# Moving the out-attention's score matmuls by a quarter of a projection, with its copies and its diagonal moved on ScalarE and GpSimd

## The chip, the cores and the metric

The kernel runs on 1 core of one Trainium2 chip. The metric is device microseconds of one execution. Five engines work beside each other, each through its own instructions in order: TensorE (PE in the profile; its weight loads are PEld), VectorE (DVE), ScalarE (ACT), GpSimd (POOL) and SyncE (SP, which here only starts transfers). They meet at semaphores: an instruction adds to one when it is done, another engine waits until it has reached a count.

## The reference

A stack of four graph layers works on 128 graphs of 64 nodes with 512 features, in float32. Layer 1, where the change lies, is

```
Wh  = x @ W[h]                      for 4 heads, 512 -> 512 each
e   = leaky(f1[:, None] + f2[None, :]),  f1 = Wh @ a[h][:512], f2 = Wh @ a[h][512:]
h   = elu(softmax(masked e) @ Wh)   heads side by side: 2048 wide
out = the same attention once more, one head, W_out: 2048 -> 512, a_out, elu
y   = relu(out @ w1 + b1) @ w2 + b2 + out, normalised, added to x, normalised
```

The first attention is the kernel's `at` (names `ah_...` in the profile), the second, the out-attention, is `ao_` (names `ao_...`).

## The kernel before, in words

A tile is 128 rows, that is two graphs; there are T = 64 tiles, worked in 32 pairs. Layer 1 runs as a pipeline over pairs: each engine has a function `step(p)`, written for p = 0 and 1, then a loop for p = 2 to 29, then p = 30 and 31. In one step TensorE aggregates and projects pair p head by head (k = 4p + head), multiplies the heads of pair p by W_out (`out_part`), and does the out-attention of the pair before, m = p - 1 (tiles 2m and 2m + 1), as well as the head attention of the pair after (tiles 2p + 2 and 2p + 3). The order on every engine is written out by hand; nothing reorders it.

TensorE's order in a step, with the lines the profile names:

- `project(p, 0, 0)`, `project(p, 0, 1)` (L2012). A projection has two quarters in each call, s = 0 and s = 1, 12 matmuls each, and ends with `h_done`.
- `out_part(m, 3, c)` (L2026), which finishes the previous pair's sums over heads in `wop` (`wo_done`); then `at.pe_scores(2p + 3)` (L212).
- `project(p, 1, 0)`; then the wait for `ao_.diag_ready` and `ao_.pe_scores(2m)` (L101); `project(p, 1, 1)`.
- `aggregate(p, 1)` (L1992), whose second bank first waits for `ao_.summed`; `out_part(p, 0, c)`; then `banks_free(p, 1)`, a wait until VectorE has read all four parts of the aggregate (`y_lo_ready`), and the turns `at.pe_turn` (L268) and `ao_.pe_turn(2m)` (L148).
- `project(p, 2, 0)`; `ao_.pe_scores(2m + 1)` (L101); `project(p, 2, 1)`; `out_sums(2m)` (L2034); `out_part(p, 1, c)`; a wait for `att_ready` and the turns of 2m + 1 and 2p + 3; `project(p, 3, *)`; `aggregate(p + 1, 0)`; `out_part(p, 2, c)`; `out_sums(2m + 1)`; `at.pe_scores(2p + 4)` (L212).

What feeds a score of the out-attention is a chain over the other engines. ScalarE copies `wop` to `who` (`keep_wo`, L1466). VectorE makes two weighted row sums of it (`out_f`, L1743 and L1747, with `ao_f` as result and `ao_.f_ready`). GpSimd spreads one of them over a diagonal (`ao_.pool_diag`, L93, `ao_.diag_ready`). TensorE then multiplies the diagonal (L101), VectorE adds, gates and masks (`dve_before_exp`, L109 to L120), ScalarE takes the exponential.

The head attention's own sums are made in between by the others: GpSimd multiplies a row tile by one of 8 vectors (`products_of`, L1300, k = 0 to 7, "product k" below), ScalarE sums each product (`dots`, L1436). There are two buffers for products, so product k waits for dot k - 2. `at.pool_diag` (L196, L199, L203) makes the head attention's diagonal, `pool_prob` (L260 for heads, L140 for the out-attention) its probabilities. In the steps p = 30 and 31 there are no products.

VectorE's order around it: `at.dve_add(2p + 3)` (L225), `out_f(2m)`, `natural` (L1765), `h_lo(k, 1)` (L1729), `ao_.dve_before_exp(2m)`, `elu(k + 1, 0)` (L1720, L1723), `at.dve_peak`, `ao_.dve_after_exp`, `elu(k + 1, 1)`, four `y_lo` (L1712), `h_lo(k + 1, 0)`, `out_f(2m + 1)`, `at.dve_after_exp`, `h_lo(k + 1, 1)`, `elu(k + 2, 0)`, `ao_.dve_before_exp(2m + 1)`, `elu(k + 2, 1)`, `out_elu(2m)` (L1753, L1756, `att_ready`). The third `y_hi` on ScalarE (L1446) waits for the first `y_lo`.

Of the kernel before, what the change touches and what calls it, by code (L numbers as in the profile page):

```python
# [415 lines left out]
def gnn_stack_kernel(nc, x, x_turned, adj, W0T, b0, Wh, ah, Wo, ao, w1, b1, w2, b2, gamma, beta,  # L416
                     W2, a2s, a2d, W3, a3s, a3d, out):
    B, N, _ = x.shape
    T = B * N // P
# [14 lines left out]
    with ExitStack() as top:  # L434
# [14 lines left out]
        same_graph = sb("same_graph", [P, P])  # L449
# [505 lines left out]
        with ExitStack() as ctx:  # L955
# [134 lines left out]
            def pair(p):  # L1090

                return not isinstance(p, int) or 0 <= p < PAIRS
# [191 lines left out]
            def _(pool):  # L1284
# [30 lines left out]
                def step(p):  # L1315
                    m = p - 1
                    first = 2 * p + 4, p + 2, 0
                    second = 2 * p + 5, p + 2, 1
                    if pair(p + 1):
                        at.pool_diag(nc, pool, 2 * p + 3, p + 1, 1, i64)  # L1320
                    if fresh(p + 2):
                        products_of(*first, range(0, 1))
                    if pair(p - 2):
                        split_att(2 * (p - 2) + 1, 1)
                    if fresh(p + 2):
                        products_of(*first, range(1, 2))
                    if pair(p + 1):
                        at.pool_prob(nc, pool, 2 * p + 2)
                    if fresh(p + 2):
                        products_of(*first, range(2, 4))  # L1330
                    if pair(m):
                        ao_.pool_diag(nc, pool, 2 * m, i64)
                    if fresh(p + 2):
                        products_of(*first, range(4, 6))
                    if pair(m):
                        ao_.pool_prob(nc, pool, 2 * m)
                    if fresh(p + 2):
                        products_of(*first, range(6, NV))
                    if pair(p + 2):
                        at.pool_diag(nc, pool, 2 * p + 4, p + 2, 0, i64)  # L1340
                    if pair(m):
                        ao_.pool_diag(nc, pool, 2 * m + 1, i64)
                    if pair(p + 1):
                        at.pool_prob(nc, pool, 2 * p + 3)
                    if fresh(p + 2):
                        products_of(*second, range(0, 2))
                    if pair(m):
                        ao_.pool_prob(nc, pool, 2 * m + 1)
                    if fresh(p + 2):
                        products_of(*second, range(2, 5))  # L1350
                    if pair(m):
                        split_att(2 * m, 0)
                    if fresh(p + 2):
                        products_of(*second, range(5, NV))
# [71 lines left out]
            def _(act):  # L1426
# [53 lines left out]
                def step(p):  # L1480
                    m = p - 1
                    k = 4 * p
                    first = 2 * p + 4, p + 2, 0
                    second = 2 * p + 5, p + 2, 1
                    if pair(m):
                        h_hi(k - 1, 1)
                    if pair(p - 2):
                        out_exp(2 * (p - 2) + 1)
                    exp(k, 0)
                    if pair(p + 1):  # L1490
                        at.act_exp(nc, act, 2 * p + 2)
                    if fresh(p + 2):
                        dots(*first, (0,))
                    if pair(p - 2):
                        split_att(2 * (p - 2) + 1, 1, p - 1)
                    exp(k, 1)
                    h_hi(k, 0)
                    if fresh(p + 2):
                        dots(*first, (1, 2))
                    if pair(m):  # L1500
                        keep_wo(m, 0)
                    h_hi(k, 1)
                    if pair(m):
                        keep_wo(m, 1)
                    if fresh(p + 2):
                        dots(*first, (3,))
                    exp(k + 1, 0)
                    if fresh(p + 2):
                        dots(*first, (4,))
                    if pair(m):  # L1510
                        ao_.act_exp(nc, act, 2 * m)
                    exp(k + 1, 1)
                    for n in range(3):
                        y_hi(p, 1, n)
                    if pair(p + 1):
                        at.act_exp(nc, act, 2 * p + 3)
                    y_hi(p, 1, 3)
                    h_hi(k + 1, 0)
                    if fresh(p + 2):
                        dots(*first, (5, 6))  # L1520
                    h_hi(k + 1, 1)
                    if pair(p + 1):
                        at.act_turned(nc, act, 2 * p + 2, p + 1, 0, agg_done)
                    if pair(m):
                        ao_.act_turned(nc, act, 2 * m)
                    if fresh(p + 2):
                        dots(*first, (7,))
                    exp(k + 2, 0)
                    if pair(m):
                        ao_.act_exp(nc, act, 2 * m + 1)  # L1530
                    if fresh(p + 2):
                        dots(*second, (0,))
                    exp(k + 2, 1)
                    if pair(m):
                        out_exp(2 * m)
                    if fresh(p + 2):
                        dots(*second, (1,))
                    h_hi(k + 2, 0)
                    if pair(m):
                        split_att(2 * m, 0, m + 1)  # L1540
                    if fresh(p + 2):
                        dots(*second, (2, 3))
                    h_hi(k + 2, 1)
                    if pair(p + 1):
                        at.act_turned(nc, act, 2 * p + 3, p + 1, 1, agg_done)
                    if pair(m):
                        ao_.act_turned(nc, act, 2 * m + 1)
                    if fresh(p + 2):
                        dots(*second, (4,))
                    exp(k + 3, 0)  # L1550
                    if fresh(p + 2):
                        dots(*second, (5,))
                    exp(k + 3, 1)
                    if pair(p + 1):
                        for n in range(3):
                            y_hi(p + 1, 0, n)
                    if fresh(p + 2):
                        dots(*second, (6,))
                    if pair(p + 1):
                        y_hi(p + 1, 0, 3)  # L1560
                    h_hi(k + 3, 0)
                    if fresh(p + 2):
                        dots(*second, (7,))
# [415 lines left out]
            def _(pe):  # L1979
# [17 lines left out]
                def banks_free(p, q):  # L1997
                    pe.wait_ge(y_lo_ready, 4 * (2 * p + q) + 4)

                def project(p, h, half):  # L2000
                    k = 4 * p + h
                    side = h % 2
                    if half == 0:
                        pe.wait_ge(y_lo_ready, 4 * (2 * p + h // 2) + 2 + 2 * side)
                    ge(pe, hv_ready, 2 * (k - 1) + half + 1)
                    for s in range(2):
                        f = slice((2 * half + s) * P, (2 * half + s + 1) * P)
                        for c in range(KC):
                            passes = split_passes(big_hi[:, h * KC + c, f], big_lo[:, h * KC + c, f],
                                                  yT[0][:, side, c, :], yT[1][:, side, c, :])  # L2010
                            for i, (a, b) in enumerate(passes):
                                ins = nc.tensor.matmul(hp[half][:, s * 2 * P:(s + 1) * 2 * P], a, b,  # L2012
                                                       start=c == 0 and i == 0, stop=c == KC - 1 and i == 2)
                    ins.then_inc(h_done, 1)
# [23 lines left out]
                def step(p):  # L2038
# [16 lines left out]
                            out_part(m, 3, c)  # L2055
                    if pair(p + 1):
                        at.pe_scores(nc, pe, 2 * p + 3, same_graph)
                    project(p, 1, 0)
                    if pair(m):
                        pe.wait_ge(at.summed, capped(2 * p + 4, T))  # L2060
                        ao_.pe_scores(nc, pe, 2 * m, same_graph)
                    project(p, 1, 1)
                    aggregate(p, 1, scores_read)
                    for c in range(KC):
                        out_part(p, 0, c)
# [3 lines left out]
                    if pair(m):  # L2069
                        ao_.pe_turn(nc, pe, 2 * m, ident)  # L2070
                    project(p, 2, 0)
                    if pair(m):
                        pe.wait_ge(ao_.turned_ready, 2 * (2 * m + 1))
                        ao_.pe_scores(nc, pe, 2 * m + 1, same_graph)
                    project(p, 2, 1)
                    if pair(m):
                        pe.wait_ge(at.turned_ready, capped(2 * (2 * p + 3), 2 * T))
                        out_sums(2 * m, 0)
# [191 lines left out]
```

## Time and profile before

| what | value |
|---|---|
| median of 3 runs | 3117.1 us (3115.95 to 3119.1) |
| the profiled execution, its own time | 3117.14 us |
| its span, first to last instruction | 3115.4 us |
| TensorE matmul, busy | 3003.0 us, 96% |
| VectorE, busy | 2262.0 us, 73% |
| GpSimd, busy | 2070.8 us, 66% |
| ScalarE, busy | 1737.4 us, 56% |
| granted TensorE clock, mean | 0.994 |

A matmul's recorded end is modelled and overlaps the next one's start, so what a stream of them takes is read from the distances of their starts. The step of pairs is the unit here: layer 1's steps repeat with the same distances, so one step is read closely and counted.

### The profile page before, as it was taken

To read this page: it belongs to the slowest core of one execution; us is meant where nothing else is said; L and a number is where in the kernel's file an instruction comes from. 1 tells how busy PE (TensorE), PEld (TensorE's weight loads), DVE (VectorE), ACT (ScalarE), POOL (GpSimd) and SP (SyncE) were. 2 spreads that over 40 slices of the span, in tenths; PEclk is the share of its full clock that TensorE was granted. 3 is DMA by queue.
4 is the path that set the end of the run, shared out by engine and by line. 5 is a ranking of instruction groups with operands and counts; after the bars stand their busy time and mean duration, and the time that the engine had idled before them with its cause. 6 is when DMAs were issued, how large, how long until landed. Compare 5 with 4: busy or idle time off the path is not lost.

```text
span 3115.4 us, 65262 instructions
## 1 busy us (share of the span) xinstructions
PE 3003.0 (96%) x19324; PEld 2656.3 (85%) x19324; DVE 2262.0 (73%) x4877; ACT 1737.4 (56%) x4250; POOL 2070.8 (66%) x2901
## 2 busy tenths in 40 slices
PE   8999989999999999999999999999799999999997
PEld 6878879888888888888888888889688888888885
DVE  7777656767676676766767667674788888888885
ACT  3333345555555555555555555553566767676675
POOL 5666656666666666666666656641588888888885
PEclk9999999999999999999999999999999999999999
DMA  6555421111111111111111111111633332333320
GB/s 200 179 187 183 148 83 34 49 51 47 44 48 49 47 47 44 53 45 47 47 44 54 44 47 47 45 50 55 193 96 95 101 93 87 99 101 99 93 74 31
DMA packets 308643, 247.65 MB, mean 79 GB/s; under 512 B 150060, under 2 KB 215644, under 8 KB 308316
## 3 DMA queue, kind: packets, MB, share of 16 engines
q1 hardware_dynamic: 296796, 221.64, 23.9%
q10 hardware_dynamic: 9216, 16.78, 1.4%
q0 software_dynamic: 2560, 8.39, 0.8%
q8 instruction: 32, 0.52, 0.1%
q14 instruction: 39, 0.32, 0.0%
HBM read 162.83 MB, written 83.91 MB: 79 GB/s over the span
## 4 chain that ended last, share of the span: by engine, by line
PE 65%; POOL 8%; issue 7%; DMA 2%; SPq 1%; DVE 1%; ACT 1%; POOLq 0%; DVEq 0%; ACTq 0%
PE wop L2026 18%; PE hp L2012 16%; PE wop L47 9%; PE hp L2145 5%; PE hp L47 5%; POOL w_first L1300 3%; PE agg L1992 2%; PE agg_b L1992 2%; DMA att_scratch<-who 2%; PE agg_b L2034 2%; PE agg_b L2112 2%; PE agg L2112 2%; SPq L1181 1%; POOL who L1305 1%; POOL g_terms L1365 1%
## 5 line engine op out<-in xcount | busy, mean ns | idle before, releaser
L1300 POOL TENSOR_TENSOR w_first<-xd,v_row 128x512 f32<-128x512 f32 x480 | 637.8, 1344 | 88.2 <-ACT w_first L1436 88.2
L2012 PE MATMUL hp<-yT_hi,big_hi 128*128 128x256 f32 x2048 | 589.8, 288 | 0.0
L2012 PE MATMUL hp<-yT_lo,big_hi 128*128 128x256 f32 x2048 | 579.3, 283 | 0.0
L2012 PE MATMUL hp<-yT_hi,big_lo 128*128 128x256 f32 x2048 | 579.0, 283 | 0.0
L1729 DVE TENSOR_TENSOR hT_lo<-ex,hT_hi 128x512 fp32r<-128x512 f32 x256 | 269.8, 1054 | 229.8 <-ACT hT_hi L1458 229.7
L2026 PE MATMUL wop<-big_hi,hT_hi 128*128 128x512 f32 x1024 | 408.3, 399 | 0.0
L2026 PE MATMUL wop<-big_lo,hT_hi 128*128 128x512 f32 x1024 | 399.9, 391 | 0.0
L2026 PE MATMUL wop<-big_hi,hT_lo 128*128 128x512 f32 x1024 | 399.9, 391 | 0.0
L2012 PEld LDWEIGHTS hp<-yT_lo,big_hi 128*128 128x128 f32 x2048 | 392.8, 192 | 0.0
L2012 PEld LDWEIGHTS hp<-yT_hi,big_hi 128*128 128x128 f32 x2048 | 392.3, 192 | 0.2
L2012 PEld LDWEIGHTS hp<-yT_hi,big_lo 128*128 128x128 f32 x2048 | 392.2, 192 | 0.0
L1436 ACT ACTIVATE w_first<-w_first 128x512 f32<-128x512 f32 x480 | 301.7, 630 | 117.2 <-POOL w_first L1300 111.2
L1365 POOL TENSOR_TENSOR g_terms<-x,g_v_row 128x512 f32<-128x512 f32 x256 | 342.2, 1357 | 33.8 <-ACT x L1587 33.8
L1458 ACT CAST hT_hi<-ex 128x512 fp32r<-128x512 f32 x256 | 158.9, 621 | 213.7 <-PE wop L2026 213.7
L1720 DVE TENSOR_SCALAR ex<-ex 128x512 f32<-128x512 f32 x256 | 125.5, 490 | 192.8 <-ACT ex L1453 191.3
L1453 ACT ACTIVATE ex<-hp 128x512 f32<-128x512 f32 x256 | 152.2, 595 | 172.1 <-PE hp L2012 169.5
L2026 PEld LDWEIGHTS wop<-big_hi,hT_hi 128*128 128x128 f32 x1024 | 192.4, 188 | 44.2
L2026 PEld LDWEIGHTS wop<-big_hi,hT_lo 128*128 128x128 f32 x1024 | 192.2, 188 | 40.7
L47 PE MATMUL wop<-w_hi,g_agg_hi 128*128 128x512 f32 x512 | 219.4, 429 | 4.5 <-DVE g_agg_lo L1836 4.3
L2026 PEld LDWEIGHTS wop<-big_lo,hT_hi 128*128 128x128 f32 x1024 | 192.5, 188 | 36.5
L47 PE MATMUL wop<-w_lo,g_agg_hi 128*128 128x512 f32 x512 | 202.3, 395 | 0.0
L47 PE MATMUL wop<-w_hi,g_agg_lo 128*128 128x512 f32 x512 | 201.7, 394 | 0.0
(219 smaller groups left out, 7969.9 us busy)
## 6 DMA issues: line engine op xcount, KB each, us to landing
x0f<-in_x_turned SPq DMA_DIRECT2D x64, 256.0 KB, 2.7
xt<-in_x SPq DMA_DIRECT2D x64, 256.0 KB, 2.9
x_scratch<-w_first ACTq DMA_DIRECT2D x64, 256.0 KB, 2.3
xa<-x_scratch SPq DMA_DIRECT2D x64, 256.0 KB, 2.7
att_hi_scratch<-att_hi SPq DMA_DIRECT2D x64, 256.0 KB, 2.0
att_lo_scratch<-who SPq DMA_DIRECT2D x64, 256.0 KB, 2.0
att_hi<-att_hi_scratch SPq DMA_DIRECT2D x64, 256.0 KB, 3.6
att_lo<-att_lo_scratch SPq DMA_DIRECT2D x64, 256.0 KB, 4.4
```

The lines of the kernel that those rows point to most:

```text
L47: ins = nc.tensor.matmul(out, a, b, start=first and c == 0 and q == 0, stop=last and c == n - 1 and q == 2)
L1300: nc.gpsimd.tensor_tensor(terms[:, k % TR, :], xd[:], v_row[:, k, :], ALU.mult).then_inc(terms_ready, 1)
L1365: nc.gpsimd.tensor_tensor(g.terms[:, k, :], x, g.v_row[:, k, :], ALU.mult).then_inc(g.terms_ready, 1)
L1436: nc.scalar.activation(terms[:, k % TR, :], terms[:, k % TR, :], ACT.Identity, accum_out=at.f[:, j, k:k + 1]).then_inc(at.f_ready[j], 1)
L1453: nc.scalar.activation(ex[half][:], hp[half][:], ACT.Exp).then_inc(ex_ready, 1)
L1458: nc.scalar.copy(hT[0][:, 2 * half:2 * half + 2, :].rearrange("p c n -> p (c n)"), ex[half][:]).then_inc(hT_hi_ready, 1)
L1720: nc.vector.tensor_scalar(ex[half][:], ex[half][:], 1.0, -1.0, ALU.min, ALU.add).then_inc(neg_ready, 1)
L1729: nc.vector.tensor_tensor(hT[1][:, own, :].rearrange("p c n -> p (c n)"), ex[half][:], hT[0][:, own, :].bitcast(F32).rearrange("p c n -> p ...
L1992: ins = nc.tensor.matmul(by_head(banks[j][:, g, :])[:, :, c, :], xa[j][own, c * P:(c + 1) * P], at.turned[own, j, 2 * q:2 * q + 2, :], sta ...
L2012: ins = nc.tensor.matmul(hp[half][:, s * 2 * P:(s + 1) * 2 * P], a, b, start=c == 0 and i == 0, stop=c == KC - 1 and i == 2)
L2026: ins = nc.tensor.matmul(wop[j][:], a, b, start=h == 0 and c == 0 and i == 0, stop=h == HEADS - 1 and c == KC - 1 and i == 2)
L2145: ins = nc.tensor.matmul(bank[:, s * 2 * P:(s + 1) * 2 * P], x, y, start=c == 0 and q == 0, stop=c == KC - 1 and q == 2)
```

## The change

Four edits.

- TensorE: `project` takes a function that it calls between its two quarters. `ao_.pe_scores(2m)` with its waits goes from before `project(p, 1, 1)` to the middle of it, and `ao_.pe_scores(2m + 1)` from before `project(p, 2, 1)` to the middle of that.
- ScalarE: in the first half of the step dot 2 moves from ahead of `keep_wo(m, 0)` to behind `keep_wo(m, 1)`, next to dot 3.
- GpSimd: `ao_.pool_diag(2m + 1)` goes ahead of `at.pool_diag(2p + 4)`.
- Nothing is added or removed: each instruction of before is issued once per step still, no transfer moves, and the epilogue behind the last step, written out apart, is as it was.

```diff
@@ GpSimd, step
                     if fresh(p + 2):
                         products_of(*first, range(6, NV))
+                    if pair(m):
+                        ao_.pool_diag(nc, pool, 2 * m + 1, i64)
                     if pair(p + 2):
                         at.pool_diag(nc, pool, 2 * p + 4, p + 2, 0, i64)
-                    if pair(m):
-                        ao_.pool_diag(nc, pool, 2 * m + 1, i64)
@@ ScalarE, step
                     if fresh(p + 2):
-                        dots(*first, (1, 2))
+                        dots(*first, (1,))
                     if pair(m):
                         keep_wo(m, 0)
                     h_hi(k, 1)
                     if pair(m):
                         keep_wo(m, 1)
                     if fresh(p + 2):
-                        dots(*first, (3,))
+                        dots(*first, (2, 3))
@@ TensorE
-                def project(p, h, half):
+                def project(p, h, half, between=None):
...
                     for s in range(2):
+                        if s == 1 and between is not None:
+                            between()
@@ TensorE, step
+                    def scores_0():
+                        if pair(m):
+                            pe.wait_ge(at.summed, capped(2 * p + 4, T))
+                            ao_.pe_scores(nc, pe, 2 * m, same_graph)
+
+                    def scores_1():
+                        if pair(m):
+                            pe.wait_ge(ao_.turned_ready, 2 * (2 * m + 1))
+                            ao_.pe_scores(nc, pe, 2 * m + 1, same_graph)
+
                     project(p, 1, 0)
-                    if pair(m):
-                        pe.wait_ge(at.summed, capped(2 * p + 4, T))
-                        ao_.pe_scores(nc, pe, 2 * m, same_graph)
-                    project(p, 1, 1)
+                    project(p, 1, 1, scores_0)
...
                     project(p, 2, 0)
-                    if pair(m):
-                        pe.wait_ge(ao_.turned_ready, 2 * (2 * m + 1))
-                        ao_.pe_scores(nc, pe, 2 * m + 1, same_graph)
-                    project(p, 2, 1)
+                    project(p, 2, 1, scores_1)
```

## Rows read from the trace of the kernel before

**Rows 1.** The profile's page, its first line.

```profile
span 3115.4 us, 65262 instructions
```

**Rows 2.** Waits of PE: us in total, times, longest us.

```profile
PE agg_b L101 <- POOL ao_diag L93: 29.3, 28, 1.1
PE agg_b L101 <- issue: 25.2, 29, 0.9
```

**Rows 3.** Windows: steps p = 1, 2 and 29, from L212 (2p + 3) to the next.

```profile
482.60:535.86 53.26, 53.26 (x387) 48.69 (x386) 38.26 (x73) 30.71 (x74) 33.12 (x36) 1.00 0.15 46
535.86:591.32 55.46, 53.54 (x387) 48.69 (x386) 38.29 (x74) 31.26 (x76) 34.93 (x37) 1.00 0.17 48
2033.14:2088.60 55.46, 53.53 (x387) 48.68 (x386) 37.75 (x74) 29.91 (x72) 31.52 (x34) 1.00 0.16 43
```

**Rows 4.** Timeline of PE in one step: start us, us, instruction, [idle before].

```profile
1534.07 0.40 PE L212 MATMUL agg_b<-ah_diag,same_graph 128*128 128x256 f32 x2
...
1536.93 0.28 PE L2012 MATMUL hp<-yT_lo,big_hi 128*128 128x256 f32 x1
1537.05 0.28 PE L2012 MATMUL hp<-yT_hi,big_lo 128*128 128x256 f32 x1
1538.38 0.43 PE L101 MATMUL agg_b<-ao_diag,same_graph 128*128 128x64 f32 x2 [1.05 <-POOL ao_diag L93]
...
1549.23 0.60 PE L268 MATMUL agg_b<-ident,ah_prob 128*128 128x128 f32 x4
...
1552.53 0.28 PE L2012 MATMUL hp<-yT_hi,big_lo 128*128 128x256 f32 x1
1553.67 0.41 PE L101 MATMUL agg_b<-ao_diag,same_graph 128*128 128x64 f32 x2 [0.86 <-issue]
...
1563.33 0.60 PE L268 MATMUL agg_b<-ident,ah_prob 128*128 128x128 f32 x4
```

**Rows 5.** Timeline of PEld behind banks_free, the same step.

```profile
1549.01 0.59 PEld L268 LDWEIGHTS agg_b<-ident,ah_prob 128*128 128x128 f32 x4
```

**Rows 6.** Timeline of ACT, the same step.

```profile
1535.09 0.63 ACT L1436 ACTIVATE w_first<-w_first 128x512 f32<-128x512 f32 x1 [2.11 <-POOL w_first L1300]
...
1557.04 0.60 ACT L1453 ACTIVATE ex<-hp 128x512 f32<-128x512 f32 x1
```

**Rows 7.** Timeline of POOL, the same step.

```profile
1533.77 1.28 POOL L1300 TENSOR_TENSOR w_first<-xd,v_row 128x512 f32<-128x512 f32 x1
1535.02 1.29 POOL L1300 TENSOR_TENSOR w_first<-xd,v_row 128x512 f32<-128x512 f32 x1
...
1538.03 0.29 POOL L93 TENSOR_TENSOR ao_diag<-i,ao_f 128x64 f32<-128x64 f32 x1 [1.73 <-DVE ao_f L1747]
...
1552.83 0.74 POOL L93 TENSOR_TENSOR ao_diag<-i,ao_f 128x64 f32<-128x64 f32 x1
```

**Rows 8.** Timeline of DVE, the same step.

```profile
1537.25 0.69 DVE L1747 CUSTOM_DVE_ANT_0 att_hi<-who,ao_row 128x512 f32<-128x512 f32 x1
...
1538.62 1.49 DVE L1729 TENSOR_TENSOR hT_lo<-ex,hT_hi 128x512 fp32r<-128x512 f32 x1
1540.04 0.21 DVE L109 TENSOR_TENSOR ao_e<-agg_b,ao_f 128x64 f32<-128x64 f32 x1
...
1547.94 0.69 DVE L1712 TENSOR_TENSOR yT_lo<-agg_b,yT_hi 128x512 fp32r<-128x512 f32 x1
...
1551.00 0.69 DVE L1747 CUSTOM_DVE_ANT_0 att_hi<-who,ao_row 128x512 f32<-128x512 f32 x1
...
1559.26 0.69 DVE L1756 TENSOR_TENSOR attT<-agg_b,attT 128x512 f32<-128x512 f32 x1
```

**Rows 9.** Timeline of DVE, then POOL, in step p = 1.

```profile
483.42 0.69 DVE L1743 CUSTOM_DVE_ANT_0 att_hi<-who,ao_row 128x512 f32<-128x512 f32 x1
...
496.11 1.65 DVE L1747 CUSTOM_DVE_ANT_0 att_hi<-who,ao_row 128x512 f32<-128x512 f32 x1
...
495.44 1.77 POOL L1300 TENSOR_TENSOR w_first<-xd,v_row 128x512 f32<-128x512 f32 x1 [2.47 <-ACT w_first L1436]
```

## The prediction

> **What bounds the kernel now.** I began with the page: TensorE's matmuls are busy for 96% of the span of 3115.4 us [rows 1], so time is only to be had where TensorE stands still. The waits say where that is: of all that TensorE waits for, the two largest entries by far belong to one line, L101, the out-attention's scores, 28 times for the diagonal and 29 times under "issue" [rows 2]. The one extra time under "issue" is in the epilogue, which the change leaves alone. Then I cut layer 1 into steps. Step p = 2 takes 55.46 us and step p = 1, which has the same matmuls, 53.26; TensorE is busy without a gap in the second number and not in the first [rows 3]. The window of step p = 29 is 55.46 us long again [rows 3], and all of the 28 steps from p = 2 to p = 29 are so to 0.02 us, so one step can be read and multiplied. The steps p = 30 and 31 have no products on GpSimd, and no such wait.
>
> In the step read closely, matmuls of a projection start 0.12 us apart. The last one ahead of the first scores starts at 1537.05, so the next could start at 1537.17, and the scores start at 1538.38: **1.21 us** lost. The second pair goes the same way: 1552.53 + 0.12 = 1552.65 against 1553.67, **1.02 us** [rows 4]. That is 2.23 us a step, near the 2.20 by which the two windows differ [rows 3]. The first scores start right behind the diagonal (1538.03 + 0.29 = 1538.32). So do the second, though the wait is put under "issue": their diagonal ends at 1552.83 + 0.74 = 1553.57 [rows 7]. Both are waits for GpSimd.
>
> **TensorE's edit.** Nothing is added; a score matmul costs the same between two quarters as between two halves. A quarter is 12 matmuls of 0.12 us, 1.44 us. In the old clock of this step, TensorE now gets to the first scores at 1537.17 + 1.44 = 1538.61. The diagonal of before was ready at 1538.32, so this edit alone removes the first stall, by 0.29 us. For the second: 1552.65 + 1.44 = 1554.09 against a diagonal at 1553.57. But TensorE will come there earlier by what the first stall gave, about 1.0 us by the sum below, so at about 1553.1; there GpSimd's edit is needed.
>
> Who waits for the scores, and for what now comes later? VectorE's L109 starts at 1540.04 [rows 8] because VectorE is busy until then; the scores would be done at about 1538.61 + 0.43 = 1539.04 [rows 4], so it does not notice. The aggregate's second bank waits for L109's sum and comes about 3 us behind the scores. Price nothing, cover 1 us and more.
>
> **ScalarE's edit.** Dot 2 stood at 1535.09 after waiting 2.11 us for product 2, with `keep_wo` behind it [rows 6]. In the new order `keep_wo` waits for `wop` alone. Step p = 1 shows what that gives, since product 2 was early there: `out_f` begins at 483.42, 0.82 us behind the start of L212 at 482.60 [rows 3, 9]. Here L212 starts at 1534.07 [rows 4], so VectorE asks for L1743 at 1534.89. Two passes of 0.69 us would then end at about 1536.3, 1.6 us earlier than the 1537.94 of before (1537.25 + 0.69 [rows 8]). It does not get that, because product 2 runs from 1533.77 to 1535.05 and product 3 follows [rows 7], and these ops do not run side by side with VectorE's ops on two SBUF operands. That is seen where L1729 takes 1.49 us [rows 8] in place of some 0.7, and where in p = 1 a product takes 1.77 us behind L1743 and L1747 then takes 1.65 us, ending at 497.76, which is 0.55 behind that product's end at 497.21 [rows 9]. So, step by step: L1743 gets in when product 2 ends and is done 0.55 behind it, at 1535.60. Product 3, held back, takes 1.1 to 1.14 us more, to 1536.74 (in p = 1, from the end of L1743 at 496.07 to 497.21). L1747 ends 0.55 behind that, at 1537.29. Against 1537.94 `ao_f` is **0.65 us earlier**, not 1.6. The bounds: 0 if the port eats it all, 1.6 if nothing collides. If product 3 got in ahead of L1743, L1747 would end 1.3 us behind 1536.30, and the shift would be about 0.35. I take 0.65, since p = 1 has exactly this pattern.
>
> The Trainium skill has this as a rule (SBUF — State Buffer, section "SBUF: two separate sides"): the port pair that VectorE and GpSimd share is an exclusive lock held for a whole instruction, and the loser blocks fully. By that rule the copy's 1.6 us shrink as worked out above; with bandwidth shared instead, nearly all of it would be kept and the time would be that of rival A.
>
> Dot 2 now runs behind the second `keep_wo`, at about 1535.8, and dot 3 behind product 3, at about 1536.8 to 1537.5. Behind them is `exp(k + 1, 0)`, for a projection that ends at 1537.3, no later than before. Products 4 and 5 wait for dots 2 and 3 but stand behind the diagonal on GpSimd anyway. Price nothing.
>
> **What is late next.** With the stall gone TensorE reaches `banks_free(p, 1)` 1.21 us earlier. Its weight load L268 starts at 1549.01 now [rows 5], and so would at 1547.80. It needs the fourth `y_lo`, which ends at 1547.94 + 0.69 = 1548.63 [rows 8]. From `out_f(2m)` to there VectorE works through its order with next to no wait, so the 0.65 us carry over: 1547.98. That is 0.18 us late, with some hundredths for the release: **a new stall of about 0.2 us**, out of the two engines' race. Its bounds are 0 (shift of 0.83 or more) and about 0.85 (no shift).
>
> **GpSimd's edit.** VectorE's second L1747 ends at 1551.00 + 0.69 = 1551.69 [rows 8], 0.65 earlier about 1551.04, and GpSimd, done with product 7 well before, makes the diagonal at once, ready by about 1551.4 (0.3 us) to 1551.8 (0.74, if it collides). TensorE comes at 1554.09 - 1.01 = 1553.08. **The 1.02 us go in full**, with over a us to spare. Without this edit the diagonal would be ready at about 1553.57 - 0.65 = 1552.9, so only just. What it delays: `at.pool_diag` starts about 1 us later than before, then `pool_prob` and products 0 and 1 of the second tile. The head diagonal is used only at the step's end. The product is awaited by a dot that stands ahead of `exp(k + 2, 1)` at 1557.04 [rows 6]; up to 0.5 us more comes onto that and onto `att_ready` (1559.26 + 0.69 = 1559.95 [rows 8]), while TensorE wants it at 1563.33 - 0.22 - 2.03, so 1561.1 [rows 4, 5]. Cover about 0.6 us left. DMA issues stay in their order and nothing of SP's is queued behind an added wait.
>
> **The sum.** Per step 1.21 - 0.2 + 1.02 = 2.03 us. Times 28: 56.8 us. Step p = 1 has no stall to give, p = 30 and 31 neither, and the epilogue stays. Off the profiled execution's own 3117.14 us (the median is 3117.1, the same): 3060.3, say **3060 us**, 1.8% faster.
>
> **Rivals.**
>
> A. The port costs less, or the wait at `banks_free` bites later than I think: both stalls go whole. 28 × 2.23 = 62.4 us, so 3055. For it: the stall I add is only 0.2 us, out of differences of modelled times. Against: the load's start, 0.22 us ahead of its matmul, is what must be met. Chance 0.2.
>
> B. VectorE gains little: product 3 gets in first, or what is won is lost again on the way to `y_lo`. With a shift of 0.35 the stall is 0.5 and the gain 1.73 × 28 = 48, so 3069; with no shift 0.85, the gain 1.38 × 28 = 39, so 3078. For it: two of VectorE's ops there collide with products (L1729 above). Against: the products behind the diagonal move with it. Chance 0.22.
>
> C. Slower: GpSimd's new order. The head diagonal and `pool_prob` now stand behind a wait for VectorE, and ScalarE's exponential stands behind the dot that follows them, so `att_ready` and with it the turns behind `out_part(p, 1)` come late. It stalls from a delay of 1559.95 to 1561.1, some 1.1 us, and turns the sum from 1.1 + 2.03 = 3.1 us on. At 4.1 us it would cost 28 × 1.0 = 28 us net, 3145. The rows give about 1 us at the source, much of it swallowed by idle time. Chance 0.03.
>
> D. No change beyond 0.2% (6 us, about what can be told from nothing): the time of a step is held by VectorE's own loop, not TensorE. The gap-free step p = 1 speaks against it, at the same VectorE busy time (38.26 against 38.29 us [rows 3]). 3117. Chance 0.04.
>
> **How the numbers follow.** Mine has 0.48, with its own range 3056 to 3066; 0.03 is left for what I do not see. The range for 8 in 10 takes A at its low end with 2 us below for terms read to hundredths, and B to its far bound: 3053 to 3079. Faster by over 0.2% holds in mine, A and B and part of the rest: 0.93. Same: 0.04. Slower: 0.03.
>
> **What would show it.** L101 no longer among TensorE's waits but for the epilogue; a step of about 53.4 us; a small wait of L268 for `yT_lo`, 28 times some 0.2 us; L1743 in the first half starting 0.8 us behind L212 and taking longer than 0.69 us by the port; product 3 at about 1.7 us; no wait at the turns behind `out_part(p, 1)`. The prediction is wrong if L268 waits for 0.5 us or more (B), if the turns wait for `att_ready` (C), or if the step stays near 55.4 with gaps elsewhere (D).

## The result, and the profile after

The changed kernel takes **3062.5 us** (median of 4 runs, 3062.35 to 3062.96) against 3117.6 us beside it (4 runs, 3115.95 to 3119.1): a ratio of 0.9824, 95% interval 0.9807 to 0.9841. Forecast were 3060 us and a range of 3053 to 3079. The span went from 3115.4 to 3060.7 us, 54.7 less. One of the runs below, of TensorE's and GpSimd's edits together, took 4214.8 us with a granted clock of 0.653, where all others have 0.993 to 0.996, and is left out of that kernel's time.

The page's first lines. Matmul busy time is hardly less than before, its share of the span is larger:

```profile
span 3060.7 us, 65262 instructions
## 1 busy us (share of the span) xinstructions
PE 2993.1 (98%) x19324; PEld 2649.7 (87%) x19324; DVE 2324.1 (76%) x4877; ACT 1726.4 (56%) x4250; POOL 2053.8 (67%) x2901
```

The waits of PE that answer to [rows 2] (us in total, times, longest us). L101 is left with the one wait of the epilogue, and a new entry stands where the forecast had put it:

```profile
PE agg_b L268 <- DVE yT_lo L1712: 7.6, 28, 0.3
...
PE agg_b L101 <- issue: 0.8, 1, 0.8
```

The windows from L212 to the next L212 that answer to [rows 3], steps p = 1 and 2, and the one read closely below:

```profile
483.21:536.24 53.03, 53.03 (x388) 48.55 (x386) 36.26 (x73) 31.22 (x76) 32.17 (x36) 1.00 0.16 46
536.24:589.76 53.52, 53.25 (x388) 48.48 (x386) 40.59 (x74) 30.89 (x76) 34.34 (x37) 1.00 0.18 50
1499.39:1552.89 53.50, 53.23 (x387) 48.47 (x386) 40.59 (x74) 30.89 (x76) 34.35 (x37) 1.00 0.18 49
```

The steps p = 2 to 29 take 1498.22 us together (536.24 to 2034.46), 53.51 each, and took 1552.74 (535.86 to 2088.60), 55.46 each. That is 54.5 us, 1.95 a step, and nearly the whole difference of the spans. A step without a gap is now seen to be 53.03, so some 0.47 us a step are still lost.

The timeline of PE in the step that begins with L212 at 1499.39, for [rows 4]; take 34.68 us off a time in those rows to compare:

```profile
1503.82 0.28 PE L2014 MATMUL hp<-yT_hi,big_lo 128*128 128x256 f32 x1
1503.94 0.33 PE L101 MATMUL agg_b<-ao_diag,same_graph 128*128 128x64 f32 x2
1504.08 0.36 PE L2014 MATMUL hp<-yT_hi,big_hi 128*128 128x256 f32 x1
1504.28 0.28 PE L2014 MATMUL hp<-yT_lo,big_hi 128*128 128x256 f32 x1
...
1513.66 0.66 PE L268 MATMUL agg_b<-ident,ah_prob 128*128 128x128 f32 x4 [0.27 <-DVE yT_lo L1712]
...
1518.57 0.33 PE L101 MATMUL agg_b<-ao_diag,same_graph 128*128 128x64 f32 x2
```

The first scores follow the quarter's last matmul at the 0.12 us of any other. The second pair starts as freely.

The timelines of DVE and, below it, of POOL in that step, for [rows 7, 8]:

```profile
1500.54 1.64 DVE L1743 CUSTOM_DVE_ANT_0 att_hi<-who,ao_row 128x512 f32<-128x512 f32 x1 [0.29 <-ACT who L1466]
1502.23 0.69 DVE L1747 CUSTOM_DVE_ANT_0 att_hi<-who,ao_row 128x512 f32<-128x512 f32 x1
...
1512.92 0.69 DVE L1712 TENSOR_TENSOR yT_lo<-agg_b,yT_hi 128x512 fp32r<-128x512 f32 x1
...
1515.99 0.69 DVE L1747 CUSTOM_DVE_ANT_0 att_hi<-who,ao_row 128x512 f32<-128x512 f32 x1
```

```profile
1500.34 1.30 POOL L1300 TENSOR_TENSOR w_first<-xd,v_row 128x512 f32<-128x512 f32 x1
...
1516.77 0.29 POOL L93 TENSOR_TENSOR ao_diag<-i,ao_f 128x64 f32<-128x64 f32 x1 [1.37 <-DVE ao_f L1747]
```

Here the trace differs from the forecast. L1743 starts 1.15 us behind L212 and not 0.82. Product 3 (1500.34) is running by then, and L1743 ends at 1502.18, 0.54 us behind that product's end. L1747 ends at 1502.92, in the old clock 1537.60 against 1537.94: the lead is 0.34 us, where the forecast's value was 0.65 and 0.35 was its bound for "product 3 got in ahead". It carries to the fourth `y_lo` unchanged: 1513.61 is 1548.29 of the old clock, against 1548.63. L268 starts 0.05 us behind it, 14.27 us behind L212. In step p = 1, where nothing holds it up, it starts 13.85 us behind. So it starts 0.42 us late, although the table of waits has 0.27: the table counts from the end given to the matmul before it (1513.01 + 0.39), and a free successor would have started 0.23 us behind that matmul's start.

### The profile page after: what moved, and what is told of

The parts are those of the page before. It is cut to its first block, busy times and chain, and to the rows that moved or that the text cites. A ratio compares the mean times of both kernels' runs of the same rounds, so it can differ in the third digit from the quotient of the medians.

```text
span 3060.7 us, 65262 instructions
## 1 busy us (share of the span) xinstructions
PE 2993.1 (98%) x19324; PEld 2649.7 (87%) x19324; DVE 2324.1 (76%) x4877; ACT 1726.4 (56%) x4250; POOL 2053.8 (67%) x2901
## 4 chain that ended last, share of the span: by engine, by line
PE 66%; DVE 9%; issue 6%; POOL 3%; ACT 2%; DMA 0%; DVEq 0%; SPq 0%; ACTq 0%; POOLq 0%
PE hp L2014 19%; PE wop L2028 18%; PE wop L47 10%; PE hp L2151 5%; PE hp L47 5%; PE agg_b L2036 2%; PE agg_b L2118 2%; PE agg L2118 2%; DVE att_hi L1743 2%; DVE hT_lo L1729 1%; DVE yT_lo L1712 1%; PE agg L1992 1%; PE agg_b L268 1%; PE agg_b L1992 1%; DVE ao_e L113 1%
## 5 line engine op out<-in xcount | busy, mean ns | idle before, releaser
L1300 POOL TENSOR_TENSOR w_first<-xd,v_row 128x512 f32<-128x512 f32 x480 | 648.4, 1369 | 74.9 <-ACT w_first L1436 74.9
L1720 DVE TENSOR_SCALAR ex<-ex 128x512 f32<-128x512 f32 x256 | 171.9, 672 | 166.6 <-ACT ex L1453 166.6
```

Source lines behind the costliest of these rows:

```text
L1300: nc.gpsimd.tensor_tensor(terms[:, k % TR, :], xd[:], v_row[:, k, :], ALU.mult).then_inc(terms_ready, 1)
L1720: nc.vector.tensor_scalar(ex[half][:], ex[half][:], 1.0, -1.0, ALU.min, ALU.add).then_inc(neg_ready, 1)
```

## Experiments

The changed kernel was taken apart by its three edits, TensorE (T), ScalarE (S) and GpSimd (G); the fourth point of the list above changes nothing. Then the 0.47 us a step that it still loses were looked for. Each run was timed against the kernel before on its chip, which took 3117.8 to 3118.1 us. Each kernel has four runs, S alone has eight. The step lengths are distances from L212 to L212.

**T alone** (`pe_only`): `project(..., between)` and the two calls in the quarters, all else as before.

> TensorE's edit alone, on the kernel before. Theory A (VectorE's lead decides): both waits for the diagonal go, since the quarter of 1.44 us covers them, but without ScalarE's edit ao_f is not the 0.34 us earlier that the changed kernel shows, so the load of L268 waits about 0.6 us in place of 0.27, 28 times. A step of about 53.85 us, 3072 us. Theory B (the moved scores do it all, the other two edits are idle): as the changed kernel, 3062 us, wait of L268 0.27.

Measured: 3077.3 us, ratio 0.9872 (0.9855 to 0.9888). Its waits of PE:

```profile
PE agg_b L268 <- DVE yT_lo L1712: 17.3, 28, 0.6
...
PE agg_b L101 <- issue: 0.8, 1, 0.8
```

0.62 us a step at L268, and none at L101: theory A, 5 us above its number. The moved scores alone take both waits off the table, as the forecast had it, and bring most of the time; what they meet at L268 depends on VectorE. The step is 54.02 us where 53.85 were expected, and the rest lies with the second scores, which still come some 0.1 us too early: their diagonal ends at 1525.96 + 0.74 = 1526.70 in the step read, and L101 starts at 1526.81 and is 0.41 us long, as where it waited. That wait is too short for the table to list.

**S alone** (`act_only`), the two lines of `dots`:

> ScalarE's edit alone. Theory A: ao_f(2m) comes 0.34 us earlier, the first stall shrinks by that, the second stays since everything ahead of it moves along: 28 times 0.34, about 10 us, 3108 us. Theory B: it gives nothing by itself, 3117.

Measured: 3108.4 us, ratio 0.9970 (0.9960 to 0.9981). Theory A to the microsecond; 29.3 us of waits for the diagonal have become 19.6, while the second scores wait as they did:

```profile
PE agg_b L101 <- issue: 25.0, 29, 0.9
PE agg_b L101 <- POOL ao_diag L93: 19.6, 28, 0.7
```

**G alone** (`pool_only`), the two lines that swap the diagonals:

> GpSimd's edit alone. Theory A: the second diagonal is ready at about 0.3 to 0.7 us behind the end of L1747, at 1552.0 to 1552.4 in the step read before, ahead of TensorE's 1552.65: the second stall goes (1.02 us and about 0.1 of restart), the first stays. 28 times 1.1, 31 us, 3086 us. Theory B: 3117.

Measured: 3085.8 us, ratio 0.9897 (0.9880 to 0.9913), theory A. Only the first wait is left:

```profile
PE agg_b L101 <- POOL ao_diag L93: 29.3, 28, 1.1
...
PE agg_b L101 <- issue: 0.8, 1, 0.8
```

This also settles what hid under "issue" in [rows 2]: GpSimd's diagonal, since moving that alone removes all 28.

**T and S** (`pe_act`):

> TensorE's and ScalarE's edits, GpSimd's order as before. Theory A: the second diagonal then ends at about 1553.57 - 0.34 = 1553.2 of the old step, just when TensorE comes: a wait of 0 to 0.2 us in the second scores, 3062 to 3068 us. Theory B: 3062. A rival on the order: GpSimd's edit also makes the later products late and costs something, so that leaving it out is faster than the changed kernel, below 3060.

Measured: 3067.3 us, ratio 0.9838 (0.9822 to 0.9854). Theory A at its upper end, 4.8 us slower than with G. No wait of L101 is recorded but the epilogue's, yet the second scores start at 1522.89, right behind a diagonal that ends at 1522.04 + 0.74 = 1522.78:

```profile
1522.89 0.41 PE L101 MATMUL agg_b<-ao_diag,same_graph 128*128 128x64 f32 x2
```

With G the same row is 0.33 us long (above). So G is worth some 5 us beside T (a step of 53.67 us against 53.51), and its reordering costs nothing that the time shows: rival C, and the rival here that leaving it out is faster, both fail.

**S and G** (`act_pool`) and **T and G** (`pe_pool`):

> ScalarE's and GpSimd's edits, TensorE as before. Theory A (without TensorE's edit the two act on two different stalls and add up, 9.6 and 32.1 us): 3076 us; L101's first wait 0.7 us each time, the second gone. Theory B (they overlap, and the second is already gone with part of the first): 3085.

> TensorE's and GpSimd's edits, ScalarE as before. Theory A: as pe_only, with L268's wait at 0.62 us 28 times, less some 0.16 us a step that the second scores still lose there, 3073 us. Theory B (GpSimd's edit gives its 32 us here too): 3046.

Measured: S and G 3077.0 us, ratio 0.9867 (0.9851 to 0.9884), so they do add up (40.9 us against 9.6 + 32.1). T and G 3072.5 us (three runs, 3072.1 to 3074.4), ratio 0.9857 (0.9837 to 0.9876), with L268's wait at 17.5 us for 28: G is worth some 5 us beside T, not 32. Theory A in both.

**Satisfied waits first** (`waits_last`), on the changed kernel:

```diff
                 def keep_wo(m, j):
-                    act.wait_ge(wo_done, 8 * m + 8)
                     if j == 0:
                         ge(act, att_stored, 4 * 16 * (2 * (m - 1) + 1))
                     ge(act, att_lo_stored, 16 * (2 * (m - 1) + j + 1))
+                    act.wait_ge(wo_done, 8 * m + 8)
...
                 def out_f(s, j, junk=junk, fresh_junk=False):
-                    dve.wait_ge(who_ready, s + 1)
                     ge(dve, ao_.diag_ready, s)
...
+                    dve.wait_ge(who_ready, s + 1)
```

> The changed kernel with the same semaphore waits in another order: keep_wo waits for wo_done last and out_f for who_ready last, so that the waits that were met long ago are passed before. Theory A (the 0.33 us by which L1743 starts later than forecast, 1.15 in place of 0.82 us behind L212, are satisfied waits issued behind the one that comes late): L1743 is asked for at 0.8 to 0.9 us behind L212, gets in ahead of product 3, L1747 ends some 0.3 us earlier and L268's wait shrinks from 0.27 to about 0; 28 times 0.3, 3054 us. Theory B (the lag has another cause): 3062 us and L1743 at 1.15 again.

Measured: 3058.3 us, ratio 0.9806 (0.9790 to 0.9823), 4.2 us under the changed kernel, half of what was expected. `keep_wo` starts 0.20 us behind L212 (0.33 before) and L1743 is asked for at 0.94 (1.15 before), so the satisfied waits were most of the lag in these steps. But 0.94 is just where product 2 ends, and the race goes either way. Two steps of this one trace, VectorE's timeline, the first begun at 748.75, the second at 1496.94:

```profile
749.69 0.69 DVE L1743 CUSTOM_DVE_ANT_0 att_hi<-who,ao_row 128x512 f32<-128x512 f32 x1
...
750.42 1.67 DVE L1747 CUSTOM_DVE_ANT_0 att_hi<-who,ao_row 128x512 f32<-128x512 f32 x1
```

```profile
1497.88 1.86 DVE L1743 CUSTOM_DVE_ANT_0 att_hi<-who,ao_row 128x512 f32<-128x512 f32 x1
...
1499.78 0.69 DVE L1747 CUSTOM_DVE_ANT_0 att_hi<-who,ao_row 128x512 f32<-128x512 f32 x1
```

and their windows:

```profile
748.75:802.08 53.33, 53.23 (x387) 48.46 (x386) 40.66 (x74) 30.88 (x76) 34.90 (x37) 1.00 0.18 49
1496.94:1550.45 53.51, 53.24 (x388) 48.47 (x387) 40.84 (x74) 30.88 (x76) 34.35 (x37) 1.00 0.18 49
```

In the first L1743 gets in ahead of product 3 and L1747 pays, the pattern of [rows 9] that the prediction had taken; the step is 53.33 us. In the second product 3 is first and the step stays at 53.51. L268's recorded wait is left in 18 steps of 28, and the order is not random: from p = 2 on it is three steps with product 3 first, three with L1743 first, then five and three by turns. What sets this rhythm was not looked for. The pattern forecast does exist, then, but it is not the one that the change gives, and it is worth less than forecast: L1747 ends at 752.09, 3.34 us behind L212 where it was 3.87 before, a lead of 0.53 and not 0.65. The ten steps account for some 1.9 us. The traced execution is 2.8 us shorter than that of the changed kernel, and step p = 1 begins 1.3 us earlier in it, for which no run shows a cause.

**No product beside `out_f`** (`port_clear`), on the changed kernel:

```diff
-                        products_of(*first, range(2, 4))
+                        products_of(*first, range(2, 3))
                     if pair(m):
                         ao_.pool_diag(nc, pool, 2 * m, i64)
                     if fresh(p + 2):
-                        products_of(*first, range(4, 6))
+                        products_of(*first, range(3, 6))
...
-                        dots(*first, (2, 3))
+                        dots(*first, (2,))
                     exp(k + 1, 0)
                     if fresh(p + 2):
-                        dots(*first, (4,))
+                        dots(*first, (3, 4))
```

> The changed kernel with product 3 behind ao_.pool_diag(2m) on GpSimd and dot 3 behind exp(k + 1, 0) on ScalarE, so that no product runs beside out_f(2m). Theory A (L1743's 1.64 us are a wait for product 3): L1743 takes 0.69, ao_f is ready about 0.95 us earlier, L268's wait goes unless product 3 collides with as much later on; 3049 to 3056 us. Theory B (out_f is slow for another reason): L1743 1.6 us again, 3062.

Measured: 3050.9 us, ratio 0.9782 (0.9766 to 0.9798), theory A. Both passes take 0.69 us with nothing else changed about them:

```profile
1493.64 0.69 DVE L1743 CUSTOM_DVE_ANT_0 att_hi<-who,ao_row 128x512 f32<-128x512 f32 x1 [0.29 <-ACT who L1466]
...
1494.38 0.69 DVE L1747 CUSTOM_DVE_ANT_0 att_hi<-who,ao_row 128x512 f32<-128x512 f32 x1
```

So 0.95 of the 1.64 us of L1743 were a wait for the product. `who` arrives as late as in the changed kernel (L1743 at 1.15 us behind L212 again), and still no wait is recorded at L268: one step is 53.10 us. There the fourth `y_lo` ends 13.80 us behind L212 and L268 starts at 13.85, as early as where nothing holds it up.

**The turns a quarter later** (`turns_mid`), on the changed kernel:

```diff
-                    banks_free(p, 1)
-                    if pair(p + 1):
-                        at.pe_turn(nc, pe, 2 * p + 2, ident)
-                    if pair(m):
-                        ao_.pe_turn(nc, pe, 2 * m, ident)
-                    project(p, 2, 0)
+                    def turns():
+                        banks_free(p, 1)
+                        if pair(p + 1):
+                            at.pe_turn(nc, pe, 2 * p + 2, ident)
+                        if pair(m):
+                            ao_.pe_turn(nc, pe, 2 * m, ident)
+
+                    project(p, 2, 0, turns)
```

> The changed kernel with banks_free(p, 1) and the two turns behind it moved into the middle of project(p, 2, 0), so that TensorE asks for the fourth y_lo 1.44 us later. Theory A (what is left is this wait alone, 0.42 us at L268 and 0.06 behind it): L268 no longer waits, a step of 53.03 us as the gap-free step p = 1, 28 times 0.48, 3049 us. Theory B: ScalarE's copies of the turned scores come 1.4 us later and make scores_1 or the exponential behind them late; a wait of L101 again, 3062 us or more.

Measured: 3049.8 us, ratio 0.9780 (0.9764 to 0.9796), theory A within a microsecond, and the fastest kernel of the study: 12.7 us under the changed one, 2.2% under the one before. TensorE is busy the whole step:

```profile
1490.05:1543.07 53.02, 53.02 (x387) 48.59 (x386) 40.16 (x74) 30.77 (x76) 34.46 (x37) 1.00 0.18 49
```

**The same without S** (`turns_no_act`):

> TensorE's and GpSimd's edits with the turns in the middle of project(p, 2, 0), ScalarE's order as before. Theory A (ScalarE's edit pays only through VectorE's lead at the fourth y_lo, which nobody waits for any more): the 0.34 us less of lead are within the 1.44 us that the later turns give, so no gap, 3050 us as with ScalarE's edit. Theory B (ScalarE's edit is worth its 15 us of pe_only against the changed kernel in itself): 3060 us or more.

Measured: 3051.6 us, ratio 0.9786 (0.9770 to 0.9802), theory A. S is worth 10 us where L268 waits (3072.5 against 3062.5) and 1.8 where it does not. Its worth was never in the copy itself.

## Why the prediction was right

**The two stalls.** Right, and undersized. The moved quarter covers the first diagonal whole and the second but for some 0.1 us (T alone), and with GpSimd's edit both. I had 2.23 us a step. Between L212 and L268 an unstalled step takes 13.85 us (483.21 to 497.06 in step p = 1 after), and it was 1549.23 - 1534.07 = 15.16 in [rows 4]: the first stall cost 1.31, not 1.21. The missing 0.1 is the restart. In [rows 4] and the rows around it, from the scores to the second matmul behind them 0.45 us pass after a wait, and 0.34 in the trace after (1503.94 to 1504.28). The second stall is short by the same 0.1 (G alone gives 1.11 us a step for its 1.02), so the whole was worth about 2.42 us a step, 55.46 - 53.03. The 2.20 us that agreed with my 2.23 in the prediction were no check: step p = 1 before was not free of gaps as I took it to be. Its scores start at 485.76 and 500.02, right behind diagonals that end at 485.61 and 499.91, and its 53.26 us are 0.23 above a free step.

**ScalarE's edit.** The mechanism was right, the size was off. Theory A's 0.34 us was seen in S alone, and `port_clear` shows what the product beside `out_f` costs. The step that failed reads: "Step p = 1 shows what that gives [...] so VectorE asks for L1743 at 1534.89". The 28 steps that count have 1.15 us there and not 0.82, so product 3 was first, which the prediction had as its bound of 0.35. `waits_last` shows that most of the difference goes with waits that are already met and stand behind the one that comes late. One would put 0.82 in p = 1 down to the waits that are not issued there, their counts being zero or less. The trace after contradicts this. In step p = 30 all of them are issued, behind the late one, and the times are those of p = 1. TensorE's, ScalarE's and VectorE's timelines there:

```profile
2034.46 0.40 PE L212 MATMUL agg_b<-ah_diag,same_graph 128*128 128x256 f32 x2
...
2034.66 0.58 ACT L1466 COPY who<-wop 128x512 f32<-128x512 f32 x1 [2.04 <-PE wop L2028]
...
2035.27 0.69 DVE L1743 CUSTOM_DVE_ANT_0 att_hi<-who,ao_row 128x512 f32<-128x512 f32 x1
```

The copy starts 0.20 us behind L212 and L1743 0.81, against 0.33 and 1.15 in the steps before. What sets p = 1 and p = 30 apart from those is that they are written out, with counts that are plain numbers, while p = 2 to 29 are one loop, whose counts follow the loop's variable. In `waits_last` p = 30 even gets worse (0.27 and 1.03). Step p = 30 has no products either, but the copy does not compete with them and shows the difference already. So the lag goes with the loop; by what it arises there no run shows.

**The new stall.** Right in place, engine, count and cause (L268 for `yT_lo`, 28 times), undersized: forecast 0.2 us, recorded 0.27, but L268 starts 0.42 us late and the step loses 0.47. By the prediction's own sum a lead of 0.35 gives a stall of 0.5, and that it comes out so near is again two misses against each other. TensorE came 1.31 us earlier and not 1.21. And it is not the load's start, 0.22 us ahead of its matmul, that the last `y_lo` has to meet: 0.05 us ahead of the matmul was early enough for L268 to start on time in `port_clear`. So the sign that I gave for rival B, a wait of 0.5 us or more at L268, was nearly met by the time lost, though not by the table.

**GpSimd's edit.** "The 1.02 us go in full" holds for the three edits together, and "without this edit [...] only just" came out slightly too good: 4.8 us are lost without it, as VectorE's lead was 0.34 and not 0.65. Rival C is not seen; no turn waits for `att_ready`, though the out-attention's probabilities (L140) do start later, 24.73 us behind L212 against 24.30 in T and S.

**The sum.** 2.42 - 0.47 = 1.95 us a step in place of 2.03. Two terms were each too small, the stalls by 0.2 and the new stall by 0.27, and nearly cancelled: that 3060 was within 3 us is partly luck. Of the rivals, A failed; B's first case is the mechanism that happened, with a time of 3062 in place of its 3069, for the stalls removed were larger as well. D fell: with TensorE's gaps gone VectorE keeps up.

## What to carry to other kernels

Where a bound engine waits briefly for a small result, put 12 of its own matmuls (1.44 us) ahead of the wait before making the producer faster: that took away each of the three waits here but for 0.16 us a step, and once the third was gone the producer's edit was worth under 2 us. A written-out step is no sure model of the steps in the loop: here the same orders began 0.13 and 0.33 us later in the loop, and the early step that passed for gap-free had lost 0.23 us of its own. Inside the loop, put the wait that comes late last, and keep an eye on which of VectorE and GpSimd gets in first, as that alone decided 0.2 us a step.

## What the runs showed of the hardware

- A stall of TensorE costs more than the gap, in the matmuls behind it: about 0.1 us at the scores (0.45 against 0.34 us from the scores to the second matmul after), some 0.05 at L268. The recorded wait is shorter than the delay, 0.27 against 0.42 us at L268 and 1.05 against 1.21 at L101.
- Satisfied semaphore waits behind a late one are not free in the steps of the loop: `keep_wo` started 0.13 us earlier there (0.33 to 0.20 behind L212) when two of them went ahead of it. In the written-out step p = 30 it started at 0.20 with the old order and at 0.27 with the new.
- Which of VectorE's pass and GpSimd's product went first was not stable within one execution once they came together: L1743 and L1747 took 0.69 and 1.67 us in 10 steps of `waits_last`, 1.86 and 0.69 in the other 18.
- A wait under "issue" in the table of waits was a wait for a GpSimd instruction 28 times of 29; and 28 waits of some 0.1 us each were not listed at all, though leaving them in costs 4.8 us over the run (`pe_act`).
